# Dividing the attention output with channels on partitions, by a matrix product that maps sums to channels

## The reference

```
x = x + attention(layernorm(x))
x = x + moe(layernorm(x))
```

## Time and profile before

| | us |
|---|---|
| median of 3 runs | 706.51 |
| lowest, highest | 700.37, 708.97 |
| the profiled execution, its own time | 704.78 |
| its span, first to last instruction | 703.0 |
| busy: PE, PEld, DVE, ACT, POOL | 664.9, 522.0, 588.0, 529.9, 477.3 |

### The profile page before, as it was taken

The page is one execution under the profiler, slowest core; times in us unless marked ns, Lnnn a source line. Parts: engine busy times, 40 slices in busy tenths (PEclk is TensorE's granted clock), DMA queues, the critical chain, the costliest instruction groups (busy, mean ns, idle before and its releaser), DMA issues.

```text
span 703.0 us, 20018 instructions
## 1 busy us (share of the span) xinstructions
PE 664.9 (95%) x6488; PEld 522.0 (74%) x6488; DVE 588.0 (84%) x1708; ACT 529.9 (75%) x1635; POOL 477.3 (68%) x599
## 2 busy tenths in 40 slices
PE   3988779999999999999999999999999999989996
PEld 2776558777777777777777777777777777767875
DVE  2688796998989798998989798998989798887763
ACT  3787767787887879787887878787887878764332
POOL 3504156877878687877878687877878687776533
PEclk9999979999999999999999999999999999999999
DMA  6010023041313214050313214050313213041321
GB/s 176 1 33 31 1 70 99 5 151 33 122 60 106 75 51 130 3 149 30 121 60 106 75 50 130 2 149 30 121 60 106 75 47 110 13 135 35 120 77 46
DMA packets 50246, 52.60 MB, mean 75 GB/s; under 512 B 5665, under 2 KB 31905, under 8 KB 50081
## 3 DMA queue, kind: packets, MB, share of 16 engines
q1 hardware_dynamic: 50208, 52.14, 24.3%
HBM read 43.20 MB, written 4.72 MB: 68 GB/s over the span
## 4 chain that ended last, share of the span: by engine, by line
PE 65%; ACT 16%; DVE 9%; issue 5%; DMA 2%; POOL 2%; DVEq 0%; POOLq 0%; ACTq 0%; SPq 0%
PE PS L1057 12%; PE PS L865 9%; PE PS L903 8%; PE PS L867 8%; PE PS L866 7%; ACT probs L603 7%; PE PS L994 5%; ACT q_by_head L554 3%; PE PS L891 3%; PE PS L1027 3%; PE PS L1054 2%; PE PS L933 2%; DVE neg_max L778 2%; DVE sums L748 2%; DVE probsT L738 1%
## 5 line engine op out<-in xcount | busy, mean ns | idle before, releaser
L603 ACT ACTIVATE probs<-PS,neg_max 128x96 f32<-128x96 f32 (+1 forms) x1024 | 247.0, 351 | 82.4 <-DVE neg_max L778 82.4
L477 POOL TENSOR_TENSOR gate<-gate,spread 128x512 f32<-128x512 f32 x124 | 158.3, 1276 | 110.4 <-ACT gate L554 49.8
L482 POOL TENSOR_TENSOR hh<-gate,tu 128x512 f32<-128x512 f32 x108 | 139.3, 1290 | 14.1 <-DVE tu L767 6.6
L1057 PE MATMUL PS<-wd,hh 128*128 128x128 f32 x1024 | 138.5, 278 | 6.9 <-POOL hh L482 4.9
L1057 PEld LDWEIGHTS PS<-wd,hh 128*128 128x128 f32 x1024 | 126.8, 192 | 15.8 <-issue 6.4
L767 DVE SCALAR_TENSOR_TENSOR tu<-th,PS 128x512 f32<-128x512 f32 x128 | 87.2, 681 | 55.3 <-ACT th L570 46.7
L778 DVE TENSOR_REDUCE neg_max<-PS 128x4 f32<-128x384 f32 (+1 forms) x256 | 121.5, 513 | 12.1 <-PE PS L903 10.8
L865 PE MATMUL PS<-x_hi,w_hi 128*128 128x512 f32 x288 | 125.2, 435 | 0.0
L570 ACT ACTIVATE th<-PS 128x512 f32<-128x512 f32 x128 | 80.4, 628 | 48.1 <-PE PS L867 46.6
L738 DVE STREAM_TRANSPOSE probsT<-probs 128x768 f32<-128x768 f32 (+1 forms) x128 | 114.5, 894 | 0.0
L867 PE MATMUL PS<-x_lo,w_hi 128*128 128x512 f32 x288 | 114.4, 397 | 0.0
(11 more groups left out here) (108 smaller groups left out, 992.2 us busy)
## 6 DMA issues: line engine op xcount, KB each, us to landing
spread<-weights_by_expert SPq DMA_DIRECT2D x248, 128.0 KB, 3.0
X<-x SPq DMA_DIRECT2D x32, 256.0 KB, 3.6
OUT<-H SPq DMA_DIRECT2D x16, 256.0 KB, 3.1
out<-OUT SPq DMA_DIRECT2D x16, 256.0 KB, 3.9
ffn_stage<-w_gu SPq DMA_DIRECT2D x1, 1152.0 KB, 7.0
wd<-w_down SPq DMA_DIRECT2D x1, 512.0 KB, 7.2
weights_by_expert<-cT SPq DMA_DIRECT2D x16, 32.0 KB, 1.6
probsT<-w_att SPq DMA_DIRECT2D x1, 192.0 KB, 3.1
```

The source lines that it names most:

```text
L477: tt(gate2[:, :], gate[:, k % 2, :], spread[:, k % SP_BUFS, :], ALU.mult).then_inc(s_g2, 1)
L482: tt(hh[:, k % 2, :], gate2[:, :], tu[:, k % 2, :], ALU.mult).then_inc(s_h, 1)
L603: ins = nc.scalar.activation(probs[:, u % PROB_BUFS, tt, 2 * rows + e, j0:KW], PS[:, rows, n * KW + j0:n * KW + KW], ACT.Exp, bias=neg_max ...
L1057: ins = mm(PS[:, 7, r], hh[:, k % 2, r], wd[:, k, :], start=(k == 0 and n == 0), stop=(k == NP - 1), skip_group_check=True)
```

## The change

The sums stay where they are, in blocks; they are inverted before they are turned, and brought to the channels instead of to the queries, so that the output is divided with channels on partitions and isn't transposed at all.

- `OT` is now stage 15 and 19: one fp32 product of 128x128 with 256 columns, `to_channel` times `by_block`. DVE multiplies it with `o_f` and writes `oT`. `ON` is gone, on PE and on ACT.
- `TURN`, stage 14 and 16: DVE takes the reciprocal of `sums` in place and turns it. `EXPAND`, stage 15 and 17, first on POOL in its step: `by_block`, the turned reciprocals spread over 8 blocks of queries and masked, 128x256.
- `PV` is (13, 13, 17, 17): all 32 small products of a sequence in one step.
- PE's waits: the first product of PV waits for the division of the sequence before to be done (it was `s_o`). The uses of the shared banks in a full slot become: s=0 LG, OW; s=1 SH, SH; s=3 OT, XT2, CT; s=4 OW, XT; s=5 QP; s=6 VP, KP; s=7 OT, XT2.
- Fill: `BUSY` 8 in place of 6, and the idle products also run in steps 0 to 3 of slot 3.
- Once, at the start: two sums on DVE for the masks `block_of` and `lane_of`, four small products on POOL for `to_channel`, ahead of `queryrow`.

```diff
-PV = (12, 13, 16, 17)
+PV = (13, 13, 17, 17)
-OT, ON, OW = 14, 15, 16
+TURN = (14, 16)
+EXPAND = (15, 17)
+OT, OW = 15, 16
-    (POST, (OT, OT + 4, ON, ON + 4, OW, OW + 4, SH)), (WEIGHTS, (CT,)))
+    (POST, (OT, OT + 4, OW, OW + 4, SH)), (WEIGHTS, (CT,)))
+def warming(slot, s):
+    return filling(slot) or slot.fixed and slot.n == 3 and s < FF % STEPS
-BUSY = 6
+BUSY = 8
...
 # POOL
+                    for b, stage in enumerate(EXPAND):
+                        g, _ = at(sl, s, stage)
+                        if g:
+                            if not (g.fixed and g.n == 0):
+                                taken(pool, slot_before(sl), (OT + 4 * b) % STEPS, POST)
+                            pool.wait_ge(s_sum_t, g.n * GB + b + 1)
+                            whole = [P, NQ, Q]
+                            tt(by_block[:, b, :, :], sums_t[:, b, :].unsqueeze(1).broadcast_to(whole),
+                               block_of[:, :].unsqueeze(2).broadcast_to(whole), ALU.mult).then_inc(s_exp, 1)
...
 # ACT
-                    g, b = at(sl, s, ON, 4, GB)
-                    if g:
-                        side, bank = filled(act, sl, s, POST)
-                        copy(oT[:, :], bank[:, 0:T]).then_inc(s_taken[side], 1)
...
 # DVE
-                            if u % 4 == 3:
-                                dve.wait_ge(s_sum, g.n * NU + u + 1)
-                                v_.transpose(sums_t[:, b, :], sums[:, b, :]).then_inc(s_sum_t, 1)
+                    def turn_sums(b):
+                        g, _ = at(sl, s, TURN[b])
+                        if g:
+                            dve.wait_ge(s_sum, g.n * NU + 4 * b + 4)
+                            link(sl, v_.reciprocal(sums[:, b, :], sums[:, b, :]))
+                            v_.transpose(sums_t[:, b, :], sums[:, b, :]).then_inc(s_sum_t, 1)
...
-                        link(sl, v_.reciprocal(o_rs[:, :, :], bank[:, T:T + Q].rearrange("p (a v) -> p a v", v=4)))
-                        v_.tensor_tensor(o_n[:, :, :].rearrange("p n (a v d) -> p (n a) v d", v=4, d=D),
-                                         bank[:, 0:T].rearrange("p (a v d) -> p a v d", v=4, d=D),
-                                         o_rs[:, :, :].unsqueeze(3).broadcast_to([P, 8, 4, D]),
-                                         ALU.mult).then_inc(s_taken[side], 1)
+                        dve.wait_ge(s_o, g.n * GB + b + 1)
+                        v_.tensor_tensor(oT[:, :], o_f[:, :], bank[:, 0:T], ALU.mult).then_inc(s_taken[side], 1)
...
+                    turn_sums(0)
                     sum_probs()
+                    turn_sums(1)
...
 # PE
-                    if filling(sl) and at(sl, s, SC, 1, NU)[0]:
+                    if warming(sl, s) and at(sl, s, SC, 1, NU)[0]:
...
-                            pe.wait_ge(s_o, g.n * GB + b)
+                            taken(pe, slot_before(sl) if b else sl, (OT if b else OT + 4) % STEPS, POST)
...
-                        pe.wait_ge(s_o, g.n * GB + b + 1)
-                        for half in range(2):
-                            nc.tensor.transpose(bank[:, P * half:P * half + P], o_f[:, P * half:P * half + P], ident)
-                        pe.wait_ge(s_sum_t, g.n * GB + b + 1)
-                        for c in range(4):
-                            ins = mm(PS[32 * c:32 * c + 32, RING[side], T:T + Q], sums_t[:, b, :], sums_of[:, c, :, :, :],
-                                     start=True, stop=True)
-                        ins.then_inc(s_filled[side], 1)
-                    g, b = at(sl, s, ON, 4, GB)
+                        if g.fixed and g.n == 0:
+                            pe.wait_ge(s_chan, 1)
+                        pe.wait_ge(s_exp, g.n * GB + b + 1)
+                        mm(bank[:, 0:T], to_channel[:, :], by_block[:, b, :, :].rearrange("p t q -> p (t q)"),
+                           start=True, stop=True).then_inc(s_filled[side], 1)
+                    g, b = at(sl, s, OW, 4, GB)
                     if g:
                         side, bank = free(POST)
-                        taken(pe, sl, (s - 1) % STEPS, POST)
-                        for half in range(2):
-                            ins = nc.tensor.transpose(bank[:, P * half:P * half + P], o_n[:, half, :], ident)
-                        ins.then_inc(s_filled[side], 1)
-                    g, b = at(sl, s, OW, 4, GB)
-                    if g:
-                        side, bank = free(POST)
-                        taken(pe, slot_before(sl) if s == 0 else sl, (s - 1) % STEPS, POST)
+                        taken(pe, sl if b else slot_before(sl), (OT + 4 * b) % STEPS, POST)
```

More of the change, by code:

```diff
@@ L220, in preln_block_kernel @@
         o_f = sb("o_f", [P, T])
-        o_rs = sb("o_rs", [P, 8, 4])
-        o_n = sb("o_n", [P, 2, P])
+        lane_of = sb("lane_of", [P, 4])
+        block_of = sb("block_of", [P, NQ])
+        to_channel = sb("to_channel", [P, P])
+        by_block = sb("by_block", [P, GB, NQ, Q])
         oT = sb("oT", [P, T])
@@ L275, in preln_block_kernel @@
         grouprow = const("grouprow")
-        sums_of = ident.rearrange("p (v h c a) -> p c h a v", v=4, h=2, c=4)
         def by_lane(n):
@@ L327, in preln_block_kernel @@
         s_sum_t = sem("sums_turned")
+        s_lane = sem("lane_masks_ready")
+        s_chan = sem("channel_map_ready")
+        s_exp = sem("reciprocals_by_block")
         s_o_ps = sem("o_in_psum")
@@ L463, in slot @@
                            ALU.subtract).then_inc(s_cst, 1)
+                    for b, stage in enumerate(EXPAND):
[7 more added lines that the diff above has]
+                               block_of[:, :].unsqueeze(2).broadcast_to(whole), ALU.mult).then_inc(s_exp, 1)
                     if sl.fixed and sl.n == 0 and s == LN1 + 1:
                         pool.wait_ge(s_w, 16 * LOADS)
+                        pool.wait_ge(s_lane, 1)
+                        for a in range(4):
+                            shape = [P, 4, D]
+                            ins = tt(to_channel[:, 32 * a:32 * a + 32].rearrange("p (v d) -> p v d", d=D),
+                                     lane_of[:, a:a + 1].unsqueeze(2).broadcast_to(shape),
+                                     grouprow.unsqueeze(2).broadcast_to(shape), ALU.mult)
+                        ins.then_inc(s_chan, 1)
                         nc.gpsimd.tensor_scalar(queryrow[:, :], headrow, Q_SCALE, 0.0, ALU.mult,
@@ L727, in slot @@
                         v_.tensor_copy(ident4[:, :], const("ident4"))
+                        v_.tensor_reduce(block_of[:, :], ident.rearrange("p (v t a) -> p t v a", t=NQ, a=HG),
+                                         mybir.AxisListType.XY, ALU.add)
+                        v_.tensor_reduce(lane_of[:, :], ident.rearrange("p (x a) -> p a x", a=HG),
+                                         AX_X, ALU.add).then_inc(s_lane, 1)
                         dve.wait_ge(s_cst, 1)
```

## The result

| | before | after |
|---|---|---|
| median, us | 703.88 (20 runs) | 711.6 (20 runs) |
| lowest, highest | 700.37, 708.97 | 704.68, 715.09 |
| profiled execution, own time; span | 704.78; 703.0 | 708.94; 707.1 |

The ratio is 1.009 with a 95% interval of 1.0062 to 1.0117 (the two medians give 1.011): the change made the kernel slower by about 1%. The forecast was 703, a little faster than the 706.5 known then, with a range of its own of 696 to 709. The time lies outside of that and inside the wider range of 688 to 714, which took in the first two rivals; it is near the 712 of the rival "slower, by the wait of LG".

A forecast was written before the change was run, and what follows sets the result against it. The bound was taken as a loop of PE, DVE and ACT, PE only a partner. 704.8 + 2.4 (0.2 a slot over twelve) - 5.0 (fill and drain) = 702.2, forecast as 703 for the median; own range 696 to 709, wider 688 to 714.

The forecast's parts named there:

- slower, by the wait of LG: Second rival, chance 0.2: LG's 0.99 goes through to the slot's end and DVE's 0.54 buys nothing; 712.
- The three pieces: A slot's loop: PE from LG to unit 2's scores, DVE to unit 5's exponentials, ACT and DVE to next LG.
- The wait of LG: Step 0: LG takes OT's bank, free only after DVE's product behind unit 7's maxima; LG 0.89 later.
- The slack of 0.28: Scores of unit 2: first rows ready 0.28 before DVE takes their maxima, so DVE is 0.71 late.
- DVE's piece: Unit 2's maxima to unit 5's exponentials: -0.73 division, +0.35 new product, -0.16 `H`'s wait; sum -0.54.
- PE's work: PE loses 0.74 a slot: twice OT's 0.60, less 0.13 for the new product and 0.1 for OW's gap.
- The burst: PV in one step: 0.80 leaves steps 0 and 4, enters 1 and 5; 0.1 counted for OW's gap.
- ACT and POOL: ACT loses two `oT` copies off the loop; POOL's `by_block`, 0.61, fits idle time, leaving 0.2 in step 1.
- Fill and drain: Kernel's start and end: clock gain 3.6, extra idle products +1.0, saved transposes 2.4; together -5.0.
- The rival by which PE is the bound: First rival, chance 0.2: the loop has unseen slack that takes LG's wait; each slot 0.74 shorter; 691.
- The rival by which the fill gains nothing: Third rival, chance 0.1: in the fill the clock falls all the same, as idle products don't bridge the waits; 706.
- The rule on tile shapes: Rival, chance 0.05: every change of tile shape costs PE 0.17, making slots 0.27 shorter; 699.

The follow-up runs named there:

- e4: Kernel before with one wait added: LG in step 0 waits until DVE has turned the exponentials of unit 6 (`probsT`); 733.68 us, ratio 1.0379.
- e5: Kernel before with one wait added: LG in step 0 waits for DVE's maxima of unit 7; 710.74 us, ratio 1.008.
- e6: Changed kernel with LG issued behind gate_up and DVE's product in step 3 moved between the maxima and `tu`; 696.31 us, ratio 0.9899 to the kernel before.
- e10: Kernel before with only PV changed, each sequence's products in one burst (13, 13, 17, 17); 705.23 us, ratio 1.0032.
- e15: Changed kernel with LG behind gate_up, DVE's product first in step 3, PV burst in step 5 only (13, 13, 16, 17); 690.96 us, ratio 0.9798.
- e2: Changed kernel with PV back in two halves (12, 13, 16, 17); 714.7 us, ratio 1.0146 to the kernel before.
- e12: Changed kernel without the new idle products, with 130 instructions of met waits ahead of PE's loop; 710.51 us, ratio 1.0082 to the kernel before.
- e18: Changed kernel with PV burst in step 5 only (13, 13, 16, 17), LG in its old place; 714.14 us, ratio 1.0103 to the kernel before.
- e1: Changed kernel with LG issued behind gate_up in step 0 and its tanh behind the gate's copy on ACT; 700.39 us, ratio 0.9937 to the kernel before.
- e3: Kernel before with only the change's idle products added (eight for six, also steps 0 to 3 of slot 3); 728.49 us, ratio 1.0339.
- e7: Changed kernel with the idle products as in the kernel before (six, filling slots only); 735.43 us, ratio 1.0457 to the kernel before.
- e11: Changed kernel with 130 more instructions of met waits ahead of PE's loop; 734.0 us, ratio 1.0405 to the kernel before.

## Why the prediction was wrong

**The step that failed** is the sum over the twelve slots: +2.4 by the forecast, +10.8 measured. It failed in two terms. The first is the slot. LG was said to be 0.89 late, of which 0.28 would vanish ahead of the maxima of unit 2, and most of the rest be met by DVE's 0.54. The three pieces, from one odd slot of each trace: LG to the maxima of unit 2, 13.47 before and 13.35 after; these maxima to the exponentials of unit 5, 15.15 and 14.74; from there to the next LG, 10.93 and 12.01. Together +0.55 in this slot, and +0.47 on the mean, where I had +0.2. The second term is the clock in the steady part, put at nothing without a reason: 4.5 in the profiled execution, and more in a typical one.

- The wait of LG was the right mechanism and a little larger than said: the last piece grew by 1.08, not 0.89.
- The slack of 0.28 was not there. In both kernels the maxima start 0.98 after the first load of the unit's mask (326.95 and 324.06), so what I took for readiness (six of eight records) was not what DVE waited for; e4 and e5 show the same by dose.
- DVE's piece gave 0.41 of the 0.54. The subtraction of step 2 and the end of `H`'s wait came as said, but L833 in step 3 is late for CT: 0.58 ahead of its load. I had counted nothing and kept 0.4 as the upper end; e6 puts it at 0.2 a slot.
- PE's work was 0.88 a slot less (38.40 for 39.28; I said 0.74), the new product 0.33 in its place, under my lower bound of 0.44. As the forecast had it, the slot didn't get shorter by it.
- The burst I treated as work moved at no cost. That is a mistake too, though one that the changed kernel doesn't pay for. The half in step 0 was a cover: PE's mask of unit 1 has to wait for the probabilities of ACT, and with the cover gone the wait stands bare (e10: 0.46, +0.5 a slot; e6 against e15: 0.52). In the changed kernel it can't be seen, because LG's own wait hides it. The loads of PE before showed a sign of it in step 1, in no row that I used:

```profile
321.38 0.10 PEld L891 LDWEIGHTS PS<-band,ident 64*128 64x128 bf16 x2 [0.36 <-ACT probs L603]
```

- The clock in the steady part was not in the forecast: three stretches at half speed, 4.5 us. Among the profiled executions, such stretches of 3.4 us stand behind LG waits of 1.23 to 1.24 (after, e2, e12, e18), and e4, which waits 1.8, has one of 6.8; the kernels whose LG waits 0.9 or less and whose loop doesn't stall have none there. That the wait brings them on is argued from this; e1, which takes the wait away, has none.
- ACT and POOL were right: `by_block` takes 0.62 and leaves 0.25 of idle time ahead of `gate2` in step 1 (0.2 said). The reciprocal and the turn cost nothing; `tu` behind them still waits for ACT.
- Fill and drain gave 6.7 (5.0 said), and the granted clock is 1.00 from 60 to 120 us. How the 6.7 divides is open: the idle products alone gave 5.3 (e3), but the burst alone, with as much half-clock time in the fill as before (17.1 us), gave 4.1 (e10). The two stretches of it that the earlier trace rows stood for:

```profile
80.00:90.00 10.00, 7.87 (x112) 6.15 (x110) 9.16 (x51) 5.49 (x21) 3.80 (x9) 1.00 0.01 3
90.00:100.00 10.00, 8.53 (x113) 6.28 (x113) 9.62 (x29) 8.19 (x31) 6.44 (x7) 1.00 0.36 110
```

With the measured sizes the sum gives the profiled execution, as it must: 704.8 + 6.3 + 4.5 - 6.7 = 708.9. The median lies 2.7 above that execution, by the clock as said above; I had put it 1.7 above. The rival "slower, by the wait of LG" named the direction and the wait, and the maxima of unit 2 that now wait 0.87 for PE bear out a part of it. But its 712 is so near to 711.6 by luck. It said that the 0.99 goes through whole and DVE's 0.54 buys nothing; the slot grew by 0.47, DVE's piece gave 0.41 back, and the slot lies between the forecast's 40.0 at most and the 40.4 at least of the rival. Half-speed stretches, which it did not have, make up the rest. The rival by which PE is the bound fails on a slot of 40.10 with 0.88 less of PE in it. The rival by which the fill gains nothing fails on its 5.8. The rule on tile shapes is left as it was: bursts change the slot by the waits that they open and close, and no run isolates a price of the change of shape.

## What to carry to other kernels

Work that is taken out of an engine's step may have been covering a wait of that engine; before counting it as saved, look whether the next instruction stands just behind a foreign result, the loads' idle times included. When a consumer is moved to another engine, look at who takes over its buffer and where in the new engine's queue it is let go; the remedy is often the order of two instructions, here LG behind gate_up and the product ahead of `tu`. One wait can hide another, so an edit that removes the hidden one measures as nothing (e18), while it is worth 0.5 once the other is gone (e6 to e15). All together were worth 1.2 a slot (40.06 to 38.89, with the wait of CT).

## What the runs showed of the hardware

- PE's loop of 1,618 or 1,702 instructions runs on without a stall or stalls in every turn, by where it begins. Packets of the instruction queue, 16 KB each: 20 or 21 in the kernels before and after and in every other run, 64 to 66 in e3, e7 and e11, some nine more for each of five turns back. The trace before has 13,718 records of PE, less five of its six turns of 1,701 some 5,210 instructions, in 20 packets: about 256 each. In stretches of 256 the loop lies over seven or over eight, depending on its place; with the code's beginning offset by anything from 19 to about 83 instructions, the loop lies over seven in the kernels with 20 or 21 packets and over eight in those with 64 to 66. That offset is fitted and no run shows it, so that seven is the limit is an inference; that the place decides is shown by e11 and e12. The price was 3.2 to 4.5 ahead of LG, once a turn of two slots, and mostly 6.8 at half clock with it (3.4 in the first turn of e7 and e11).
- The Trainium skill, Runtime: NRT & Kernel Launch, Instruction fetch mechanics, gives TensorE an instruction memory of 128 KiB, 2,048 instructions, refilled in blocks of 16 KiB. By my estimate from these figures a loop over eight such blocks would fill it whole, and one over seven leaves one free, which goes with the limit inferred above. The section doesn't state such a limit. The same section says that the memory is only two lines and that a taken branch outside of them fetches its target; by that every kernel here would fetch in every turn, and most do not.
- A wait of PE of 1.23 to 1.24 ahead of LG, in every second slot, is followed now and then by 3.4 us at 1.2 GHz in a part in which PE is otherwise busy: three times in the changed kernel's profiled execution, five in e18's, once in those of e2 and e12. Each costs about 1.5. e18's times go with it: 705.4 at a mean granted clock of 0.998, 718.3 at 0.981. The kernel before, without such a wait, varies with its clock too (beside e10 from 699.1 at 0.993 to 708.5 at 0.983), so this isn't the only source.
